# Attention: rows of maxima issued from ScalarE's queue, experts' chunks asked for in the last groups

## The chip, the cores and the metric

One Trainium2 chip, one core of it. The metric is the time on the device of one launch, in microseconds (us). TensorE does matmuls and transposes, VectorE and ScalarE elementwise work and reductions, GpSimd (POOL) some elementwise work and indirect transfers; SyncE (SP) issues nearly all DMAs. Each engine runs its own instructions in order and waits on semaphores for the others; all DMAs, whoever issues them, move through the same 16 DMA engines.

## The reference

Six layers in one launch on x of 4 images, 256 channels, 16 x 16: a deformable convolution block, a selective scan block, attention, a mixture of experts, causal attention, a second mixture of experts. What matters here is the attention, of which there are two, the second causal:

```
q, k, v = split(x @ w_qkv)              # 4 images x 16 heads, 256 tokens, head width 16
scores  = q @ k^T                       # causal in the second
attn    = softmax(scores / sqrt(16))
out     = (attn @ v) @ w_proj + b_proj
```

and that each attention is followed by 8 experts (hidden width 512 after the first attention, 1024 after the second), two of which are chosen for every token. The experts' weights are read from HBM in chunks of 1,536 KB: one per expert in the first mixture, two in the second. A ring in SBUF holds six chunks.

## The kernel before, in words

**Groups and units.** The 64 pairs of image and head are cut into 8 groups (`GROUPS`) of 8 pairs, a group into 4 units (`UNITS`) of 2 pairs. Unit i belongs to group i // 4. The softmax needs the maximum of each row of scores. A first pass computes scores (TensorE, line 1539, `scores_for_max`), whose maxima VectorE takes (line 1353; line 1348 in the causal attention). This pass runs ahead of the rest by up to two groups.

**Rows of maxima.** When the maxima of a group are complete, TensorE turns them (line 1549, `turn_maxima`) into a bank of PSUM; ScalarE writes their negative in bf16 (line 1439, `negate`), then VectorE writes the remainder (line 1359, `negate`). The result, two rows, is copied by two DMAs of 4 KB (8 pieces of 512 bytes each) into two extra rows of `stack_q` (line 1307, `load_max_rows`). There the second pass (line 1564, `scores_less_max`) subtracts them as part of the matmul. In the kernel before, GpSimd issues these two DMAs. Groups complete at units 2 (group 1), 4 (group 2), 8, 12, 16, 20 and 24 (group 7); group 0 before the first unit. Only the first unit of a group waits for the rows of that group, so those sent at unit 8 are needed at unit 12; those of group 1, sent at unit 2, are needed at unit 4.

**A unit.** For each unit TensorE computes the scores less the maxima, ScalarE exponentiates them (line 1463). In the causal attention GpSimd then zeroes the future (line 1313), in the same queue as the DMAs of line 1307. TensorE weighs the values for two units at a time (line 1584). In the first unit of a group ScalarE, after its exponential, takes the contexts of the group before out of PSUM (line 1444, `take_contexts`); TensorE turns them in the second unit (line 1595, `turn_contexts`), VectorE divides them (lines 1366 and 1368, `divide`), TensorE turns them back in the third (line 1602) and, for every second pair of groups, projects in the fourth (line 1612). The order of every engine's work is written out by hand in loops over `g` and `unit`.

**SyncE.** At the start of each group g, when its first unit's scores are done, SyncE issues one chunk of the experts' weights (line 1291, `prefetch`, line 1665), while there are chunks wanted: three in the first attention (groups 0 to 2), six in the second (groups 0 to 5). Then, in groups 1 to 4, it issues the 12 DMAs of 64 KB of the stacks of group g + 3 (line 1273, `load_stacks`). The first four groups' stacks are issued ahead of that loop (line 1283).

Of the kernel before, what the change touches and what calls it, by code (L numbers as in the profile page):

```python
# [1117 lines left out]
STACK = len(COMBOS) * HD  # L1118
MAXROWS = 2
GROUP = 8  # L1120
GROUPS = B * AH // GROUP
SLOTS_G = 4
# [25 lines left out]
def maxima_ahead(i):  # L1148


    catching_up = GROUP // 2
    first = FIRST_MAXIMA + 3 * min(i, catching_up) + 2 * max(i - catching_up, 0)
    return range(first, min(first + (3 if i < catching_up else 2), GROUP * GROUPS))


def maxima_complete(i):

    for g in range(1, GROUPS):
        if i > 0 and GROUP * g + GROUP - 1 in maxima_ahead(i - 1):
            return g  # L1160
    return 0


def attention(nc, sem, sbuf, psum, k, w, causal, tag, prefetch):
# [12 lines left out]
    with ExitStack() as ctx:  # L1177
# [16 lines left out]
        stack_q = sb("stack_q", [STACK + MAXROWS, SLOTS_G, GROUP, N], BF16)  # L1194
# [3 lines left out]
        negated = sb("negated", [GROUP, SLOTS_G, MAXROWS, N], BF16)  # L1198
# [26 lines left out]
        s_nh = sm("negated_high")  # L1225
        s_nl = sm("negated_low")
        s_mr = [sm("max_rows_even"), sm("max_rows_odd")]
# [31 lines left out]
        @block.sync  # L1259
        def _(sp):  # L1260
            for dst, src in ((wqkv, w["wqkv"]), (w_proj, w["w_proj"]), (b_proj, w["b_proj"])):
                sp.dma_start(dst[:], src).then_inc(s_w, 16)
            if causal:
                sp.dma_start(later[:], k.dram["later"]).then_inc(s_w, 16)

            sp.dma_start(stack_k[STACK:].rearrange("r s h n -> r (s h n)"), k.dram["ones16"]).then_inc(s_ones_rows, 16)

            def load_stacks(g):

                b, half = image_and_half(g)  # L1270
                for which, stack in enumerate((stack_q, stack_k)):
                    for c, combo in enumerate(COMBOS):
                        sp.dma_start(stack[c:STACK:len(COMBOS), g % SLOTS_G],
                                     parts[:, half, which, combo[which], N * b:N * b + N]).then_inc(s_st[g % SLOTS_G], 16)

            for g in range(SLOTS_G):
                b, t = image_and_half(g)
                for which in range(2):
                    for part, done in enumerate((s_hi, s_mid, s_lo)):
                        sp.wait_ge(done, 2 * t + which + 1)  # L1280
                        for c, combo in enumerate(COMBOS):
                            if combo[which] == part:
                                sp.dma_start((stack_q, stack_k)[which][c:STACK:len(COMBOS), g],
                                             parts[:, t, which, part, N * b:N * b + N]).then_inc(s_first[g], 16)
            sp.wait_ge(s_lo, SPLITS)

            for g in range(GROUPS - 1):

                sp.wait_ge(s_s2, UNITS * g + 1)
                prefetch(sp, g)  # L1290
                if g >= 1 and g + 3 < GROUPS:

                    load_stacks(g + 3)

        @block.gpsimd
        def _(pool):
            pool.memset(values[:, :, :, HD:], 1.0).then_inc(s_ones, 1)
            pool.wait_ge(s_ones, 1)
            pool.wait_ge(s_w, 16 * WEIGHTS)
            pool.wait_ge(ln.s_out, TT)  # L1300
            pool.tensor_tensor(k.t[:], k.t[:], b_proj[:].unsqueeze(1).broadcast_to([P, TT, C]), ALU.add).then_inc(s_bias, 1)

            def load_max_rows(g):
                pool.wait_ge(s_nl, g + 1)
                pool.wait_ge(s_nh, g + 1)
                for q in range(MAXROWS):
                    pool.dma_start(stack_q[STACK + q:STACK + q + 1, g % SLOTS_G], negated[:, g % SLOTS_G, q, :]  # L1307
                                   ).then_inc(s_mr[g % 2], 16)

            def zero_future(i):  # L1310
                pool.wait_ge(s_ex, i + 1)
                on_diagonal = exponentials(i).rearrange("p j (m n) -> p j m n", m=NT)[:, :, :, 0:P]
                pool.affine_select(on_diagonal, on_diagonal, [[0, 2], [0, NT], [1, P]], ALU.is_ge, 0.0, base=0,
                                   channel_multiplier=-1).then_inc(s_sel, 1)

            if causal:
                load_max_rows(0)
                for i in range(UNITS * GROUPS):
                    zero_future(i)
                    if maxima_complete(i + 1):  # L1320
                        load_max_rows(maxima_complete(i + 1))
            else:
                for g in range(GROUPS):
                    load_max_rows(g)

        @block.vector
        def _(dve):
# [75 lines left out]
        @block.scalar  # L1403
        def _(act):
            ln.deviation(act)

            def take_turned(i):
                act.wait_ge(s_ht, i + 1)
                act.activation(h_t[:, :, N * i:N * i + N], psum[:, 4 + i, :].rearrange("p (t n) -> p t n", t=CT),
                               ACT.Copy).then_inc(s_hto, 1)  # L1410

            def split(i):
                act.wait_ge(s_qk, i + 1)
                act.activation(part_of(i, 0), psum[:, split_bank(i), :], ACT.Copy).then_inc(s_hi, 1)
                act.wait_ge(s_r, i + 1)
                act.activation(part_of(i, 1), rest[:, i % 2, 0:BANK], ACT.Copy).then_inc(s_mid, 1)

            def take_values(i):

                act.wait_ge(s_v, i + 1)  # L1420
                act.activation(values[:, 2 * i:2 * i + 2, :, 0:HD],
                               psum[:, 4 + i, :].rearrange("p (a h d) -> p a h d", a=2, h=AH), ACT.Copy).then_inc(s_vo, 1)

            take_turned(0)
            take_turned(1)
            split(0)
            split(1)
            take_turned(2)
            take_turned(3)
            split(2)  # L1430
            split(3)
            take_values(0)
            take_values(1)
            for i in range(SPLITS // 2, SPLITS):
                split(i)

            def negate(g):
                act.wait_ge(s_mt, g + 1)
                act.activation(negated[:, g % SLOTS_G, 0, :], psum[0:GROUP, 0, 0:N], ACT.Copy, scale=-1.0).then_inc(s_nh, 1)

            def take_contexts(g):

                act.wait_ge(s_av, QUADS * (g + 1))
                act.activation(raw[:, g % 2, :], psum[:, 6 + g % 2, :], ACT.Copy).then_inc(s_raw, 1)

            def take_back(g):

                b, half = image_and_half(g)
                act.wait_ge(s_cb, g + 1)
                act.activation(ctxn[:, b % 2, half, :], psum[:, 6 + g % 2, 0:N], ACT.Copy).then_inc(s_cn, 1)  # L1450

            negate(0)
            for i in range(TT // 4, TT // 2):
                take_values(i)
            for g in range(GROUPS):
                for unit in range(UNITS):
                    i = UNITS * g + unit
                    if maxima_complete(i):
                        negate(maxima_complete(i))
                    act.wait_ge(s_s2, i + 1)  # L1460
                    if i >= 4:
                        act.wait_ge(s_av, i // 2 - 1)
                    act.activation(exponentials(i)[:, :, 0:WIDTH], psum[:, 2 + 2 * (i % 2):4 + 2 * (i % 2), 0:WIDTH],
                                   ACT.Exp, scale=HD ** -0.5).then_inc(s_ex, 1)
                    if unit == 0 and g >= 1:
                        take_contexts(g - 1)
                    if unit == 2 and g >= 1:
                        take_back(g - 1)
            take_contexts(GROUPS - 1)
            take_back(GROUPS - 1)  # L1470

# [189 lines left out]
def load_chunk(sp, k, weights, chunks, n, loaded):  # L1661

    place = CHUNK_COLS * (n % RING_CHUNKS)
    column = CHUNK_COLS * (n % chunks)
    sp.dma_start(k.ring[:, place:place + CHUNK_COLS], weights[n // chunks, :, column:column + CHUNK_COLS]).then_inc(loaded, 16)
# [612 lines left out]
def build(nc, k, out):  # L2278

    with ExitStack() as ctx:  # L2280
# [29 lines left out]

        def prefetcher(name, chunks, wanted, loaded):

            def prefetch(sp, i):
                if i < len(wanted):
                    load_chunk(sp, k, k.dram[name], chunks, wanted[i], loaded)
            return prefetch

        with nc.cleanup_on_exit():
# [39 lines left out]
```

## Time and profile before

| | |
|---|---|
| runs of the kernel, us | 1013.53, 1019.27, 1018.63 (median 1018.63) |
| the profiled execution, us | 1018.52 |
| its span, us | 1016.8 |
| mean granted clock of TensorE | 0.896 |
| busy share of the span | PE 82%, DVE 45%, ACT 30%, POOL 23% |
| DMA | 80.39 MB, mean 79 GB/s |

The span goes from the first to the last instruction of the profiled execution. Shares are averages over six layers with different limits; the two attentions lie between 257 and 388 us and between 577 and 694 us of the span. The granted clock is a fraction of TensorE's full speed; its two levels are 2.4 GHz (1.00) and 1.2 GHz (0.50).

### The profile page before, as it was taken

What the parts mean: (1) busy time and instruction counts of PE and PEld (TensorE: products, weight loads), DVE (VectorE), ACT (ScalarE), POOL (GpSimd) and SP (SyncE); (2) the same over time, 40 slices, a digit from 0 to 9 for tenths busy, and PEclk for the clock granted to TensorE, in tenths of its full rate; (3) what the DMA queues carried; (4) which work ended last, traced back from release to release, by engine and by line L of the source; (5) the groups of instructions that cost most, each with busy time, mean ns of one, the idle gap of its engine ahead of it and who ended that gap; (6) DMA issues with size and microseconds to landing.
All of it is one profiled execution on the core that took longest, in us unless ns stands there. A gap on an engine that the chain in (4) does not pass through costs nothing. (4 is left out here: it accounts for less than half of the span.)

```text
span 1016.8 us, 12888 instructions
## 1 busy us (share of the span) xinstructions
PE 837.7 (82%) x4088; PEld 538.6 (53%) x4089; DVE 452.6 (45%) x1165; ACT 301.3 (30%) x478; POOL 233.3 (23%) x314
## 2 busy tenths in 40 slices
PE   3769379899887986599999387876499999999993
PEld 2768237435743545366666344555356666666652
DVE  4974631698775645422222566645412121211213
ACT  3223235632244562012212144452021212222221
POOL 1150000573200100334433113340212211122110
PEclk8579677999898997699999597898699999999996
DMA  3000070000136503042111436832003007600003
GB/s 110 1 1 1 1 259 1 0 1 0 54 97 185 147 6 92 21 128 79 46 46 36 146 82 190 245 109 91 16 16 146 26 26 275 261 22 29 21 21 129
DMA packets 53621, 80.39 MB, mean 79 GB/s; under 512 B 10021, under 2 KB 45989, under 8 KB 50373
## 3 DMA queue, kind: packets, MB, share of 16 engines
q1 hardware_dynamic: 48040, 67.37, 20.5%
q0 software_dynamic: 5536, 12.46, 4.1%
q8 instruction: 24, 0.39, 0.2%
q14 instruction: 21, 0.16, 0.1%
HBM read 55.82 MB, written 11.27 MB: 66 GB/s over the span
## 5 line engine op out<-in xcount | busy, mean ns | idle before, releaser
L2096 PE MATMUL psum<-ring,f_x_t 128*128 x552 | 248.6, 593 | 1.3 <-DVE f_x_t L1961 1.3
L1954 DVE TENSOR_TENSOR f_gated<-f_silu,psum 128x512 f32<-128x512 f32 x69 | 47.5, 688 | 265.4 <-PE psum L2096 265.4
L2096 PEld LDWEIGHTS psum<-ring,f_x_t 128*128 128x128 f32 x552 | 99.5, 190 | 100.9 <-issue 100.8
L2110 PE MATMUL psum<-ring,f_gated_t 128*128 x552 | 130.7, 380 | 1.8 <-ACT f_gated_t L2020 1.8
L2110 PEld LDWEIGHTS psum<-ring,f_gated_t 128*128 128x128 f32 x552 | 101.2, 190 | 23.4 <-issue 12.7
L2020 ACT ACTIVATE f_gated_t<-psum 128x512 f32<-128x512 f32 x69 | 41.2, 597 | 235.0 <-PE psum L2103 231.5
L2016 ACT ACTIVATE f_silu<-psum 128x512 f32<-128x512 f32 x69 | 41.2, 597 | 116.5 <-PE psum L2096 109.8
L1114 PE MATMUL psum<-ident_sb 128*128 128x128 f32 x188 | 33.5, 347 | 30.8 <-PEq L2325 16.7
L1822 POOL COPY f_from_now<-f_from_row 128x1 uint32 (+1 forms) x48 | 9.0, 187 | 207.6 <-PE psum L2089 204.0
L1825 POOL DMA_INDIRECT f_xs<-rows_in,f_from_now x48 | 47.5, 989 | 36.5 <-POOL f_from_now L1822 36.5
L1834 POOL DMA_INDIRECT rows_out<-f_y,f_to_now x46 | 46.0, 1001 | 36.4 <-POOL f_to_now L1831 31.4
L1539 PE MATMUL psum<-a_stack_k,a_stack_q 96*128 96x256 bf16 (+1 forms) x256 | 43.3, 275 | 13.2 <-DVE a_maxima L1348 5.7
L1114 PEld LDWEIGHTS psum<-ident_sb 128*128 128x128 f32 x188 | 31.6, 260 | 32.7 <-issue 25.1
L1353 DVE TENSOR_REDUCE a_maxima<-psum 128x2 f32<-128x512 f32 x64 | 41.0, 686 | 11.9 <-PE psum L1539 11.9
L1564 PE MATMUL psum<-a_stack_q,a_stack_k 98*128 98x256 bf16 (+1 forms) x256 | 37.9, 275 | 8.8 <-DMA a_stack_q<-a_negated 7.3
L1307 POOL DMA_DIRECT2D a_stack_q<-a_negated x32 | 16.8, 530 | 120.5 <-DVE a_negated L1359 120.5
L1348 DVE CUSTOM_DVE_ANT_0 a_masked<-psum,a_later 128x128 bf16<-128x128 f32 (+1 forms) x128 | 38.1, 353 | 12.5 <-PE psum L1539 12.4
L719 POOL TENSOR_TENSOR u<-dtb,ring 128x512 f32<-128x512 f32 x32 | 40.4, 1268 | 13.2 <-ACT dtb L907 13.0
L2103 PE MATMUL psum<-ident_sb,f_gated 128*128 128x128 f32 x276 | 41.5, 273 | 1.3 <-DVE f_gated L1954 1.3
L1539 PEld LDWEIGHTS psum<-a_stack_k,a_stack_q 96*128 96x128 bf16 x256 | 20.9, 102 | 37.0 <-DVE a_maxima L1353 11.0
L802 DVE TENSOR_TENSOR_SCAN state<-psum,u 128x512 f32<-128x512 f32 x32 | 38.9, 1217 | 3.0 <-POOL u L719 3.0
L2103 PEld LDWEIGHTS psum<-ident_sb,f_gated 128*128 128x128 f32 x276 | 34.4, 141 | 9.1 <-DVE f_gated L1954 2.4
(295 smaller groups left out, 1259.1 us busy)
## 6 DMA issues: line engine op xcount, KB each, us to landing
ring<-in_f_experts SPq DMA_DIRECT2D x24, 1536.0 KB
a_stack_q<-a_parts SPq DMA_DIRECT2D x96, 64.0 KB, 2.0
a_stack_k<-a_parts SPq DMA_DIRECT2D x96, 64.0 KB, 2.0
rows_in<-h SPq DMA_DIRECT2D x4, 1024.0 KB, 5.8
ring<-rows_out SPq DMA_DIRECT2D x8, 512.0 KB, 5.8
a_wqkv<-in_a_wqkv SPq DMA_DIRECT2D x2, 768.0 KB, 4.4
x_in<-in_x SPq DMA_DIRECT2D x1, 1024.0 KB, 4.9
out<-x SPq DMA_DIRECT2D x4, 256.0 KB, 2.1
```

What stands on the lines that cost most here:

```text
L719: pool.tensor_tensor(u[:, i % DEEP, :], dtb[:, i % DEEP, :], x_perm[:, h, BANK * half:BANK * half + BANK], ALU.mult).then_inc(s_u, 1)
L1114: pe.matmul(bank[:, 0:P], k.ident_sb[:], k.ident_sb[:], start=True, stop=True)
L1353: dve.tensor_reduce(maxima[:, g, :, h], psum[:, i % 2, :].rearrange("p (t m) -> p t m", t=NT), AX_X, ALU.max).then_inc(s_mx, 1)
L1539: last = pe.matmul(out, stack_q[0:STACK, slot, h, P * t:P * t + P], stack_k[0:STACK, slot, h, 0:keys], start=True, stop=True)
L1825: pool.indirect_dma_start(out=xs[:, odd, :], out_offset=None, in_=k.rows_in, in_offset=bass.IndirectOffsetOnAxis(ap=from_now[:, odd:odd + ...
L1834: pool.indirect_dma_start(out=k.rows_out, out_offset=bass.IndirectOffsetOnAxis(ap=to_now[:, odd:odd + 1], axis=0), in_=y[:, odd, :], in_of ...
L1954: dve.tensor_tensor(gated[:, b, :], silu[:, b, :], psum[:, 2 * b + 1, :], ALU.mult).then_inc(s_g, 1)
L2016: act.activation(silu[:, b, :], psum[:, 2 * b, :], ACT.Silu).then_inc(s_si, 1)
L2020: act.activation(gated_t[:, b, :], psum[:, G_BANK + b, :], ACT.Copy).then_inc(s_gto, 1)
L2096: last = pe.matmul(psum[:, 2 * b + side, :], x_t[:, xb, t, :], k.ring[:, bass.ds(at + start, CHUNK)], start=(t == 0), stop=(t == CT - 1))
L2103: last = pe.transpose(psum[:, G_BANK + b, P * a:P * a + P], gated[:, b, P * a:P * a + P], k.ident_sb[:])
L2110: last = pe.matmul(psum[:, Y_BANK, 0:C], gated_t[:, b, P * a:P * a + P], k.ring[:, bass.ds(at + start, C)], start=(c == 0 and a == 0), sto ...
```

## The change

Two edits. First, the two DMAs of the rows of maxima are issued by ScalarE, directly after its `negate`, and no longer by GpSimd. For that ScalarE waits for VectorE's part (`s_nl`) before it issues them, and its exponential of that unit stands behind. This is so for group 0 ahead of the loop, and at units 2, 4, 8, 12, 16, 20 and 24, in both attentions. Second, SyncE asks for no chunk in groups 0 to 3; in groups 4, 5 and 6 it asks for a third of the wanted chunks each, one in the first attention and two in the second, and in group 4 behind the stacks of group 7.

```diff
@@ sync
                 sp.wait_ge(s_s2, UNITS * g + 1)
-                prefetch(sp, g)
                 if g >= 1 and g + 3 < GROUPS:
 
                     load_stacks(g + 3)
+                if g >= GROUPS - 4:
+                    prefetch(sp, g - (GROUPS - 4))
@@ gpsimd
-            def load_max_rows(g):
-                pool.wait_ge(s_nl, g + 1)
-                pool.wait_ge(s_nh, g + 1)
-                for q in range(MAXROWS):
-                    pool.dma_start(stack_q[STACK + q:STACK + q + 1, g % SLOTS_G], negated[:, g % SLOTS_G, q, :]
-                                   ).then_inc(s_mr[g % 2], 16)
...
             if causal:
-                load_max_rows(0)
                 for i in range(UNITS * GROUPS):
                     zero_future(i)
-                    if maxima_complete(i + 1):
-                        load_max_rows(maxima_complete(i + 1))
-            else:
-                for g in range(GROUPS):
-                    load_max_rows(g)
@@ scalar
+            def load_max_rows(g):
+                act.wait_ge(s_nh, g + 1)
+                act.wait_ge(s_nl, g + 1)
+                for q in range(MAXROWS):
+                    act.dma_start(stack_q[STACK + q:STACK + q + 1, g % SLOTS_G], negated[:, g % SLOTS_G, q, :]
+                                  ).then_inc(s_mr[g % 2], 16)
...
             negate(0)
+            load_max_rows(0)
             for i in range(TT // 4, TT // 2):
                 take_values(i)
...
                     if maxima_complete(i):
                         negate(maxima_complete(i))
+                        load_max_rows(maxima_complete(i))
                     act.wait_ge(s_s2, i + 1)
@@ build
         def prefetcher(name, chunks, wanted, loaded):
 
+            each = len(wanted) // 3
+
             def prefetch(sp, i):
-                if i < len(wanted):
-                    load_chunk(sp, k, k.dram[name], chunks, wanted[i], loaded)
+                for n in wanted[each * i:each * i + each]:
+                    load_chunk(sp, k, k.dram[name], chunks, n, loaded)
```

## Rows read from the trace of the kernel before

**Rows 1.** Busy time of each engine (x instructions), granted clock, DMA share, GB/s: two attentions.
```profile
288.00:388.00 100.00, 80.26 (x636) 46.59 (x635) 56.28 (x101) 49.34 (x68) 8.48 (x16) 0.95 0.36 102
577.00:694.00 117.00, 94.13 (x722) 60.64 (x722) 67.39 (x332) 51.76 (x86) 35.02 (x50) 0.88 0.51 148
```

**Rows 2.** Who waited for whom, TensorE, 304:366 us: total, times, longest.
```profile
PE psum L1564 <- DMA a_stack_q<-a_negated: 4.5, 2, 3.5
```

**Rows 3.** The same view, TensorE, 615:675 us.
```profile
PE psum L1564 <- DMA a_stack_q<-a_negated: 2.8, 2, 1.5
PE psum L1539 <- DMA a_stack_k<-a_parts: 1.2, 2, 0.7
```

**Rows 4.** Windows from one turning of maxima to the next, first attention, columns as rows 1.
```profile
309.44:318.49 9.05, 4.63 (x38) 2.29 (x39) 4.14 (x7) 2.30 (x3) 1.03 (x2) 0.95 0.55 190
318.49:328.77 10.28, 8.83 (x74) 4.71 (x73) 5.97 (x11) 5.33 (x7) 1.03 (x2) 0.83 0.75 225
328.77:337.98 9.21, 8.62 (x74) 4.47 (x73) 5.97 (x11) 5.33 (x7) 1.03 (x2) 0.87 0.90 256
...
357.22:365.37 8.15, 7.40 (x72) 4.28 (x73) 6.54 (x12) 5.20 (x7) 1.03 (x2) 1.00 0.01 1
```

**Rows 5.** The same windows in the second attention.
```profile
619.25:627.07 7.82, 5.68 (x39) 2.78 (x40) 4.10 (x25) 1.87 (x3) 2.33 (x4) 0.50 0.64 219
627.07:637.03 9.96, 7.98 (x75) 5.02 (x74) 5.71 (x35) 4.47 (x7) 3.59 (x6) 0.78 0.84 232
637.03:647.24 10.21, 8.88 (x74) 5.63 (x72) 5.71 (x35) 4.35 (x7) 3.59 (x6) 0.67 0.88 239
...
665.26:673.22 7.96, 6.18 (x72) 3.85 (x72) 6.21 (x36) 4.35 (x7) 3.59 (x6) 1.00 0.60 209
```

**Rows 6.** DMA issues, KB each, us to landing, window 309:320 us.
```profile
a_stack_q<-a_negated POOLq DMA_DIRECT2D x2, 4.0 KB, 5.6
```

**Rows 7.** DMA issues, the same columns, window 343:350 us.
```profile
a_stack_q<-a_negated POOLq DMA_DIRECT2D x2, 4.0 KB, 1.8
```

**Rows 8.** DMA queues, packets, MB, share of 16 engines, window 310.5:316.5 us.
```profile
q1 hardware_dynamic: 257, 1.62, 77.1%
```

**Rows 9.** SyncE's queue in order of time: start us, us, what.
```profile
309.84 9.22 SPq L1665 DMA_DIRECT2D ring<-in_f_experts  x2
...
350.77 5.00 SPq L1273 DMA_DIRECT2D a_stack_k<-a_parts  x6
...
388.21 0.43 SPq L1781 DMA_DIRECT2D f_iota_e<-in_iota_e  x1
388.69 0.42 SPq L1781 DMA_DIRECT2D f_iota_b<-in_iota_b  x1
```

**Rows 10.** SyncE's queue, second attention, the last stacks and the last chunk.
```profile
660.47 4.68 SPq L1273 DMA_DIRECT2D a_stack_k<-a_parts  x6
665.19 0.59 SPq L1665 DMA_DIRECT2D ring<-in_f_experts  x1
```

**Rows 11.** ScalarE in order of time at unit 16 of the first attention [idle <-releaser].
```profile
348.08 0.37 ACT L1439 ACTIVATE a_negated<-psum 8x256 bf16<-8x256 f32 x1 [2.69 <-PE psum L1549]
348.36 1.00 ACT L1463 ACTIVATE a_expo<-psum 128x1024 f32<-128x1024 f32 x1
349.26 0.57 ACT L1444 ACTIVATE a_rest<-psum 128x512 f32<-128x512 f32 x1
```

**Rows 12.** VectorE at the same unit.
```profile
348.49 0.41 DVE L1359 SCALAR_TENSOR_TENSOR a_negated<-psum,a_negated 8x256 bf16<-8x256 f32 x1 [0.88 <-ACT a_negated L1439]
```

**Rows 13.** TensorE: contexts turned; first scores of group 6.
```profile
349.92 0.62 PE L1595 MATMUL psum<-ident_sb,a_rest 128*128 128x128 f32 x4
...
364.41 0.60 PE L1564 MATMUL psum<-a_stack_q,a_stack_k 98*128 98x256 bf16 x4
```

**Rows 14.** TensorE in the second attention, values weighed at unit 18.
```profile
660.11 0.86 PE L1584 MATMUL psum<-a_expo,a_values 128*32 128x256 f32 x16 [0.18 <-POOL a_expo L1313]
```

**Rows 15.** A window of 3 us, first attention, columns as rows 1.
```profile
318.00:321.00 3.00, 3.00 (x23) 1.10 (x22) 0.41 (x1) 1.28 (x2) 0.73 (x2) 0.51 0.43 127
```

## The prediction

> **What bounds the kernel now.** The change touches the two attentions only, so I read the busy times by stage first: the two take about 100 and 117 us, TensorE is busy for 80.3 and 94.1 us of them, and the mean granted clock is 0.95 and 0.88 [rows 1]. Then the waits of TensorE inside the loops: it waited 4.5 us for the rows of maxima in the first attention (twice, the longest 3.5), 2.8 us in the second, and 1.2 us there for stacks [rows 2, 3]. Then the length of one group, from one turning of maxima to the next. A group without projection takes 8.15 us in the first attention when no transfer is in its way, at a full clock; those that begin at 318.49 and 328.77 take 10.28 and 9.21 at a mean clock of 0.83 and 0.87 [rows 4]. In the second the like are 7.96 against 9.96 and 10.21, at 0.78 and 0.67 [rows 5]. So the early groups lose time to DMA waits and to the lower of TensorE's two levels, which follows such waits: after the wait of 3.5 us the clock was 0.51 for 3 us [rows 2, 15].
>
> Why the rows of maxima come late is in the issues: beside a chunk the two DMAs of 4 KB landed 5.6 us after issue, beside stacks alone 1.8 us [rows 6, 7]. In 6 us SyncE's queue moved 1.62 MB, with all 16 engines busy 77.1% of it, so a chunk holds them for some 4.6 us [rows 8].
>
> **Step 1, chunks out of groups 0 to 3.** The first attention gets back the wait of 3.5 us before its second group, 10.28 - 8.15 = 2.1 and 9.21 - 8.15 = 1.1 [rows 2, 4]: 6.7 us. The second gets back 2.8 - 1.5 = 1.3 before its second group, 9.96 - 7.96 = 2.0 and 10.21 - 7.96 = 2.2 [rows 3, 5]: 5.5 us. Sum -12.2. The bounds: the waits alone, 4.5 + 2.8 + 1.2 = -8.5, if the lower clock stays; and -13.7, if the second attention's first window, all of it at 0.50, gives 1.5 us more [rows 5]. I take -12.2, since the undisturbed groups show the length that is left.
>
> The Trainium skill (DMA: Bandwidth & Descriptors, Queues, rings and completion order) says that each DMA engine goes round the queues it has work for, a packet at a time. By that the small rows should slip in between a chunk's packets; landings of 5.6 against 1.8 us don't look like it, unless a packet is a large part of a chunk. Its consequence is the third rival.
>
> **Step 2, two DMAs on ScalarE.** Unit 16 shows the chain. ScalarE's negation starts at 348.08, the exponential at 348.36, the contexts leave PSUM from 349.26 to 349.83 [rows 11]; TensorE turns them at 349.92 [rows 13]: slack 0.09. In the changed kernel ScalarE waits for VectorE's remainder, which ends at 348.49 + 0.41 = 348.90 [rows 12], 0.54 after the old start of the exponential, and then issues two DMAs. No row shows a DMA issued by ScalarE. Lower bound: the 0.05 us between two issues of SyncE (388.21 + 0.43 to 388.69); upper bound: a stack's issue with its gap, 0.64 (5.00 us for six is more still) [rows 9, 10]. The nearest is SyncE's small load, 0.43 + 0.05 = 0.48, but in four of six groups SyncE is issuing stacks at that moment; I take 0.55. The hold is 0.54 + 2 x 0.55 = 1.64, less the slack 1.55 us.
>
> I find no cover behind it. TensorE stands at the turning of contexts, and in its queue behind it the next scores for maxima; VectorE's division waits for that turning, with its next maxima queued behind; ScalarE's next exponential stands behind the taking of contexts. So TensorE, VectorE and ScalarE are all 1.55 us later at the next turning of maxima. It happens at units 4, 8, 12, 16, 20 and 24, six times in each attention: 12 x 1.55 = +18.6. Units 2 and the one ahead of the loop I cost at nothing: there the contexts aren't on the path, and the next copy or exponential on ScalarE waits for TensorE anyway; without that cover they cost 4 x 1.6 = 6.4. Bounds of the step: 12 x (0.54 + 0.1 - 0.09) = +6.6, and 12 x (0.54 + 1.28 - 0.09) = +20.8. Less than nothing is excluded: a wait and two issues can't make the exponential earlier.
>
> GpSimd loses 16 issues in each attention. In the second they stand ahead of the zeroing of the future, for which TensorE waited 0.18 us [rows 14]; but the exponential that feeds it is now 1.6 us later, so I count nothing.
>
> By the Trainium skill (Perfetto Trace Analysis, DMA Instruction — HWDGE) two sequencers share one descriptor generator under a lock, and the one that waits for it is held. No row here shows such a wait. By that rule each of ScalarE's DMAs could wait out one of SyncE's.
>
> **Step 3, chunks into groups 4 to 6.** In the second attention SyncE issues stacks until 665.15 and its next chunk follows at 665.19 [rows 10], when group 5 has begun. So the two chunks of group 4 and the two of group 5 are now asked for together, and two more a group later. Four chunks hold the DMA engines for 4 x 4.6 = 18 us [rows 8]; the rows of groups 6 and 7 are sent in that time and have some 6 to 7 us until they are needed (first attention: turned at 357.22, so sent about 358.9, and needed at 364.41 plus the hold [rows 4, 13]). Landing 5.6 us after issue costs nothing; if each of the two DMAs waits for a chunk of its own they land after about 10 us, 3 late. In the first attention two chunks stand where four do, about 1 late. Bounds 0 and +20 (all four chunks first). I take +4, near the landings seen. The blocks of experts begin only behind the attentions, at 388 and 694 [rows 1], and 18 us from 665 is 683, so the later chunks delay nobody.
>
> **Sum.** -12.2 + 18.6 + 4 = +10.4. The profiled execution took 1018.52, a tenth under the median of 1018.63; its span is 1016.8. Forecast 1018.5 + 10.4 = 1029 us.
>
> **Rivals.**
> 1. *The issue is cheap on ScalarE* (the other side). If a DMA costs it 0.05 and not 0.55 us, step 2 is +6.6; with step 1 at -13.7 and no collision late, the time is 1018.5 - 7.1 = 1011, and with -12.2 and +4 it is 1017. It decides below 0.12 us an issue: 12 x (0.45 + 2 x 0.12) = 8.2 is what steps 1 and 3 leave. For it: the chain has only 0.09 us of slack but all issues measured here are another engine's. Against: even SyncE's small loads take 0.42 us [rows 9]. Chance 0.22.
> 2. *Dearer still.* Each DMA of ScalarE waits 0.6 us for one of SyncE's in groups 1 to 4, 8 x 1.2 = +10; or the new gaps of 1.5 us put TensorE on its lower level, which doubles some 1 us of work in each of 12 groups. 1039 to 1045. The clock fell after a wait of 3.5 us [rows 15] but not in the undisturbed groups; a gap of 1.5 lies between. Chance 0.22.
> 3. *Queues take turns.* Then the slow landings come from GpSimd's own path; moving the rows to ScalarE cures them just as well, and step 3 is 0: 1025. Its contrary, strict order behind four chunks, gives +20: 1045. Chances 0.06 each; rows 6 and 7 speak against the first.
> 4. *The hold is absorbed somewhere I haven't seen* and only step 1 remains: 1006. Chance 0.06.
>
> **How the numbers follow.** The forecast, 1020 to 1038, has 0.38. A measurement of this kernel can tell about 1% from no change, that is 1008 to 1029. Faster by over 1%: rival 4 and the best third of rival 1, 0.13. Slower by over 1%: about 0.21 of the forecast, all of rival 2 and half of rival 3's cases, 0.49, cut to 0.47 for the unknown price of an issue. Within 1%: 0.40. The range leaves out rival 4 with the edge of rival 1, and the far end of rivals 2 and 3: 1009 to 1042.
>
> **What would show it.** In the changed trace: landings of the rows near 2 us in groups 1 to 5, no wait of the scores less maxima at groups 1 and 2, and a full clock there (step 1); two DMA rows on ScalarE between line 1439 and line 1463, their length, and a wait of line 1595 for line 1444 of about 1.5 us in twelve groups (step 2); groups of 9.7 us where 8.15 stood; a wait of groups 6 and 7 for the rows of maxima (step 3). The prediction is wrong if the exponential starts less than 0.8 us after its old place, or if undisturbed groups grow by less than 1 us.

## The result, and the profile after

The changed kernel takes 1035.3 us (median of four runs, 1034.3 to 1039.4) beside 1016.9 for the kernel before; the ratio is 1.019, with an interval of 1.015 to 1.024. The forecast was 1029: the sign and the hold on ScalarE came out, but of the 18.4 us only 10.4 were forecast, and the lower clock that follows the hold was not in the sum. The profiled executions, 1039.39 and 1018.52 us, lie 20.9 apart (the one of the changed kernel is the slowest of its four, with a mean granted clock of 0.890 where the others have 0.895 to 0.901), and the attentions hold it all: from the first turning of maxima (line 1549 before, 1546 after) to the experts' first load the first attention goes from 87.9 to 95.2 us and the second from 84.3 to 98.8, while the last mixture of experts takes 322.2 and 321.8.

ScalarE, then TensorE, at unit 16 of the first attention, in the changed kernel (start us, us, what, [idle before <-releaser]; compare [rows 11, 13]):

```profile
350.67 0.37 ACT L1427 ACTIVATE a_negated<-psum 8x256 bf16<-8x256 f32 x1 [2.69 <-PE psum L1546]
351.57 1.29 ACTq L1433 DMA_DIRECT2D a_stack_q<-a_negated  x2
352.96 1.02 ACT L1460 ACTIVATE a_expo<-psum 128x1024 f32<-128x1024 f32 x1 [1.92 <-PE psum L1561]
353.88 0.59 ACT L1439 ACTIVATE a_rest<-psum 128x512 f32<-128x512 f32 x1
```

```profile
352.07 0.60 PE L1561 MATMUL psum<-a_stack_q,a_stack_k 98*128 98x256 bf16 x4
354.53 0.66 PE L1592 MATMUL psum<-ident_sb,a_rest 128*128 128x128 f32 x4 [1.86 <-ACT a_rest L1439]
```

The exponential started 0.28 us after the negation and now starts 2.29 after it; between them are 0.53 of wait and 1.29 of issues. The idle time in the exponential's row is put down to TensorE's scores, but those of its unit were done by 349.5: a releaser that has long been done isn't the one; what ended last is the engine's own queue of DMAs. TensorE stands 1.86 us before it can turn the contexts. Over both loops this is the largest of its waits (total, times, longest); what else is listed are waits for VectorE's maxima and small ones of at most 1.0 us. No wait for the rows of maxima or for stacks is left, where there were 4.5, 2.8 and 1.2 us [rows 2, 3]. First attention 305:390, then second 615:702; of the eight waits in the first, six are at the turnings forecast and two behind them (0.17 and 0.72 us):

```profile
PE psum L1592 <- ACT a_rest L1439: 12.5, 8, 2.3
```

```profile
PE psum L1592 <- ACT a_rest L1439: 11.1, 6, 2.5
```

The groups, from one turning of maxima to the next (TensorE, its loads, VectorE, ScalarE, GpSimd busy, granted clock, DMA share, GB/s), answer to [rows 4, 5]. The second and third row are groups with and without projection at a full clock; the last two are groups with and without projection in the second attention, both below a full clock:

```profile
327.30:338.85 11.55, 9.00 (x72) 4.81 (x73) 6.07 (x11) 5.23 (x7) 0.00 (x0) 0.85 0.27 69
338.85:350.25 11.40, 8.81 (x80) 5.96 (x80) 6.16 (x11) 5.23 (x7) 0.00 (x0) 1.00 0.28 71
...
363.26:373.24 9.98, 7.42 (x72) 4.36 (x72) 6.63 (x12) 5.23 (x7) 0.00 (x0) 1.00 0.47 181
```

```profile
666.23:679.98 13.75, 10.53 (x81) 7.30 (x81) 6.30 (x36) 4.38 (x7) 2.55 (x4) 0.75 0.56 178
679.98:690.56 10.58, 7.60 (x73) 4.75 (x73) 6.22 (x36) 4.38 (x7) 2.55 (x4) 0.84 1.01 431
```

At a clock of 1.00 a group has grown from 8.15 to 9.98 us [rows 4], by 1.83: the hold and no more. Beside it stand groups of 11.55 and 13.75 us at 0.85 and 0.75, with TensorE busy for 9.00 us where the group of 9.98 has 7.42 for the same work. That is the second part of the loss, and the forecast had it only as a rival. SyncE's queue shows where the six chunks went: asked for from 673.46 on, behind the last stacks, four of them by 680.0 and the last two at 690.2.

```profile
669.41 4.00 SPq L1273 DMA_DIRECT2D a_stack_k<-a_parts  x6
673.46 17.50 SPq L1662 DMA_DIRECT2D ring<-in_f_experts  x6
```

### The profile page after: what moved, and what is told of

Same layout as the page of the kernel before. It is cut to its first block and busy times, and to the rows that moved or that the text cites. A ratio compares the mean times of both kernels' runs of the same rounds, so it can differ in the third digit from the quotient of the medians.

```text
span 1037.7 us, 12885 instructions
## 1 busy us (share of the span) xinstructions
PE 846.8 (82%) x4088; PEld 543.5 (52%) x4089; DVE 453.6 (44%) x1165; ACT 301.7 (29%) x478; POOL 216.4 (21%) x282
## 5 line engine op out<-in xcount | busy, mean ns | idle before, releaser
L1810 POOL TENSOR_TENSOR f_label_hot<-f_in_block,f_labels 128x192 bf16<-128x192 f32 x8 | 7.8, 1002 | 169.7 <-DVE f_in_block L1914 169.7
L1561 PE MATMUL psum<-a_stack_q,a_stack_k 98*128 98x256 bf16 (+1 forms) x256 | 40.5, 290 | 1.4 <-ACT a_values L1409 1.4
```

The lines of the kernel that those rows point to most:

```text
L1561: last = pe.matmul(psum[:, bank, col:col + N - first], stack_k[:, slot, h, P * m:P * m + P], stack_q[:, slot, h, first:N], start=True, sto ...
```

## The experiments

The theory was made from the traces of the two kernels, before the runs below. Theory *hold*: ScalarE's wait and two issues ahead of the exponential delay TensorE in twelve groups, and the gaps bring the lower clock with them. Rivals: the chunks in the last groups are the loss; the wait across engines and not the issue; the lower clock has another cause. Times are medians; the kernel before, on the same chip, was 1016.2, 1016.0 and 1015.6 us in the three sets (kernels 1 to 4, 5 to 8, 9 to 11).

**1. The queue alone.** The changed kernel, with the chunks as before the change. Here and below `...` marks lines left out within an edit, and the lines that only change how `prefetch` picks its chunks aren't shown.

```diff
+                prefetch(sp, g)
                 if g >= 1 and g + 3 < GROUPS:
                     load_stacks(g + 3)
-                if g >= GROUPS - 4:
-                    prefetch(sp, g - (GROUPS - 4))
```

> The rows of maxima are issued by ScalarE as in the changed kernel, but the chunks are asked for as before the change. Theory hold (the exponential stands behind ScalarE's wait and its two issues, 1.85 us in each of 12 groups, and the lower clock that follows takes the rest): the hold is all there, the chunks still delay the rows of the second group (up to 3.5 us), later waits are covered by the longer groups; 4 to 9 us slower than the changed kernel, 1039 to 1045. Rival late chunks (the six chunks in the last groups are what costs): this kernel loses that cost and lands at 1017 to 1027.

Measured 1045.8 us, ratio 1.026 (1.020 to 1.032), just above what was expected. The rival's 1017 to 1027 is far off, so the chunks aren't the loss. That the queue alone costs more than the whole change is likely and no more: three of its four runs took 1045 to 1047, one 1036.8, and the intervals of the two ratios overlap. Beside a chunk ScalarE's rows come late too: TensorE waits for them at group 1, 2.2 us in the first attention (305:390) and 1.2 in the second, where the changed kernel has no such wait.

```profile
PE psum L1560 <- DMA a_stack_q<-a_negated: 2.2, 1, 2.2
```

The rows of this wait were issued at 311.67. ScalarE's DMAs have a queue of their own in the trace, q10; all its 32 packets of these two rows start in 315.7:317.3, none in 311.67:315.7, while q1, SyncE's queue, moves the chunk (packets, MB, share of 16 engines):

```profile
q1 hardware_dynamic: 110, 1.35, 88.3%
```

```profile
q10 hardware_dynamic: 32, 0.01, 2.2%
```

**2. The chunks alone.** The other half of the change: GpSimd issues the rows, SyncE's lines are those of the changed kernel.

> GpSimd issues the rows of maxima as before the change; only the chunks are moved into groups 4 to 6. Theory hold: the waits of 4.5 and 4.0 us and the lower clock behind them go, 1003 to 1008, with groups of 8.1 us in the first attention. Rival late chunks: slower than before, 1020 or more, with waits for the rows in groups 6 and 7. Rival (the slow landings are GpSimd's own path): landings stay at 5 us and the time at 1015 to 1019.

Measured 1013.0 us, ratio 0.996 (0.994 to 0.998): a gain, but 5 us less than expected. The early groups of the first attention came out as forecast (8.14 and 8.55 us at a clock of 1.00). In the second the first two windows keep the lower clock, 0.51 and 0.78, though no wait for rows or stacks stands there. The last groups now wait for the rows of maxima. TensorE's waits, second attention, 669:696:

```profile
PE psum L1565 <- DMA a_stack_q<-a_negated: 4.4, 2, 3.5
```

and one group, in which TensorE waited 1.8 us for stacks, stands at a clock of 0.75:

```profile
638.48:651.94 13.46, 10.64 (x80) 7.19 (x81) 5.71 (x35) 4.36 (x7) 3.60 (x6) 0.75 0.28 71
```

**3. ScalarE's issues moved behind the contexts.** The changed kernel with

```diff
                         negate(maxima_complete(i))
-                        load_max_rows(maxima_complete(i))
+                        if i == 2:
+                            load_max_rows(1)
...
                     if unit == 2 and g >= 1:
                         take_back(g - 1)
+                        if g + 1 < GROUPS:
+                            load_max_rows(g + 1)
```

> The changed kernel, but from group 2 on ScalarE issues the two rows in the third unit of the group, after it has taken the contexts back, and not ahead of the exponential of the first unit; the rows are sent some 4 us later. Theory hold: TensorE's wait of 1.85 us at the turning of contexts goes in all twelve groups, 1004 to 1012, with perhaps a short wait for the rows at each group's start. Rival (any DMA issue on ScalarE costs its 1.3 us wherever it stands, since ScalarE is full): 1025 or more.

Measured 1027.5 us, ratio 1.011 (1.008 to 1.014): a miss by 15 us, in the range that was given to the rival. The trace speaks against the rival all the same. The wait for the contexts is gone, as the theory has it; but rows sent 4 us later land late, above all beside the chunks, which I hadn't priced: TensorE waits 6.2 us for them in the first attention and 13.0 in the second. TensorE's waits in the second attention, 615:702:

```profile
PE psum L1564 <- DMA a_stack_q<-a_negated: 13.0, 5, 6.2
...
PE psum L1595 <- ACT a_rest L1439: 0.7, 1, 0.7
```

**4. The wait without the issues.** Kernel 2, with ScalarE waiting for VectorE's remainder.

```diff
                         negate(maxima_complete(i))
+                        act.wait_ge(s_nl, maxima_complete(i) + 1)
```

> GpSimd issues the rows and the chunks are late (as in the kernel with only the chunks moved), but ScalarE waits for VectorE's remainder before its exponential and issues nothing. It parts the hold into wait and issue. Theory hold, by its parts (0.54 of wait, 2 x 0.64 of issue, 0.09 of slack): 12 x 0.5 = 6 us over the kernel with only the chunks moved, 1009 to 1014, TensorE's wait at the turning of contexts about 0.6 us. Rival (it is the wait across engines, not the issue, that costs): as slow as the changed kernel, 1030 or more.

Measured 1016.4 us, ratio 1.000 (0.998 to 1.001), 3.4 over kernel 2, where 6 was expected, and above the interval expected. TensorE's wait for the contexts (305:390) is 0.42 us at each plain turning, where about 0.6 was expected; a part of it comes back, as the longer groups leave the rows more time (3.1 us of waiting where kernel 2 had 4.1 there).

```profile
PE psum L1597 <- ACT a_rest L1445: 3.3, 6, 0.9
PE psum L1566 <- DMA a_stack_q<-a_negated: 3.1, 2, 2.9
```

**5. TensorE kept busy in the gap.** The changed kernel, with 12 transposes of the identity, into a bank that is overwritten later, ahead of the wait for the contexts in groups 1 to 6.

```diff
+            def keep_busy(g):
+                if g >= 2:
+                    pe.wait_ge(s_cn, g - 1)
...
+                square_identity(pe, k, psum[:, 6 + g % 2, :], 12)
...
                     if unit == 1 and g >= 1:
+                        if g < GROUPS - 1:
+                            keep_busy(g)
                         turn_contexts(g - 1)
```

> The changed kernel, in which TensorE runs 12 transposes of the identity (about 1.5 us at the higher clock, into a bank that is overwritten later) in the second unit of groups 1 to 6, where it would stand and wait for the contexts. They fill the gap of 1.85 us and change nothing of the order. Theory clock (the gaps bring TensorE to its lower level in the groups that follow, which the trace of the changed kernel shows as 0.75 to 0.87): the clock returns to 1.00, groups 4 and 5 of the second attention shrink from 13.5 to about 11, and the kernel gains 8 to 15 us on the changed kernel, 1020 to 1028. Rival (the lower clock has another cause, and the groups are long by the hold alone): the fillers cost or give nothing, 1033 to 1040.

Measured 1030.9 us, ratio 1.014 (1.010 to 1.018): outside the interval expected, 4.4 us less than the changed kernel. The clock is 1.00 in the whole first attention, and in the second but for its first three windows (0.83, 0.51 and 0.83), but twelve transposes took some 2.6 us and overran the gap: a group with projection took 11.99 where the changed kernel has 11.40.

**6. One row each.** The changed kernel, with the second row issued by GpSimd, with a semaphore of its own.

```diff
@@ scalar
-                for q in range(MAXROWS):
+                for q in range(1):
@@ gpsimd
+            def load_second_row(g):
+                pool.wait_ge(s_nl, g + 1)
+                pool.wait_ge(s_nh, g + 1)
+                pool.dma_start(stack_q[STACK + 1:STACK + 2, g % SLOTS_G], negated[:, g % SLOTS_G, 1, :]
+                               ).then_inc(s_mr2[g % 2], 16)
...
```

> The changed kernel, but ScalarE issues one of the two rows and GpSimd the other. Theory hold, by its parts: ScalarE's hold is shorter by one issue of 0.64 us, TensorE's wait at the turning of contexts 1.2 instead of 1.85 us, 12 x 0.64 = 7.7 us less, and more if the clock is lost only behind the longer gap: 1020 to 1028. Rival (the first DMA of ScalarE carries the cost, the second is cheap): 1032 or more.

Measured 1024.1 us, ratio 1.008 (1.005 to 1.010), as expected: 11.2 us less than the changed kernel, 12 x 0.64 = 7.7 for the issues, the rest by the clock, if theory and kernel 9 hold. Its gaps are 1.20 us and not 1.86, and the clock of all full groups of the first attention is 1.00 (9.32 us without projection, 10.73 with it); in the second three of five are at 1.00. ScalarE at unit 16 (344.51 its negation): the hold is shorter by one issue.

```profile
344.51 0.37 ACT L1440 ACTIVATE a_negated<-psum 8x256 bf16<-8x256 f32 x1 [2.69 <-PE psum L1559]
345.41 0.63 ACTq L1446 DMA_DIRECT2D a_stack_q<-a_negated  x1
346.14 1.02 ACT L1473 ACTIVATE a_expo<-psum 128x1024 f32<-128x1024 f32 x1 [1.26 <-PE psum L1595]
```

**7. Rows by SyncE**, but for group 0's; chunks when the last rows have landed.

```diff
                 sp.wait_ge(s_s2, UNITS * g + 1)
+                sp.wait_ge(s_nh, g + 2)
+                sp.wait_ge(s_nl, g + 2)
+                for q in range(MAXROWS):
+                    sp.dma_start(stack_q[STACK + q:STACK + q + 1, (g + 1) % SLOTS_G], negated[:, (g + 1) % SLOTS_G, q, :]
+                                 ).then_inc(s_mr[(g + 1) % 2], 16)
...
```

> SyncE issues the rows of groups 1 to 7, ahead of each group's stacks, GpSimd those of group 0; all chunks are asked for when the rows of the last group have landed. SyncE's 12 stacks take 7.6 us or more of a group of 8; with the wait for the remainder (1.5 us) and 1.3 us for the rows its queue needs 10.5 us a group in groups 1 to 4. Theory (SyncE's queue becomes the bound): waits for stacks in groups 2 to 5 of both attentions, 5 to 12 us more than with GpSimd's issues, 1008 to 1018. Rival (its queue has room): as fast as the kernel with the chunks last, 1000 to 1006.

Measured 1018.9 us, ratio 1.003 (1.001 to 1.005), one above the interval expected and 9.5 us slower than kernel 8, which differs from it only in who issues the rows. SyncE becomes the bound; TensorE in the second attention (615:702):

```profile
PE psum L1545 <- DMA a_stack_k<-a_parts: 6.6, 3, 2.8
```

It also prices the disputed DMA on another engine. All 28 on SyncE, then all 32 on ScalarE in the changed kernel (ns, min/median/max):

```profile
L1294 SPq DMA_DIRECT2D a_stack_q<-a_negated x28: 623/686/732, 310.2 to 674.4; - x28
```

```profile
L1433 ACTq DMA_DIRECT2D a_stack_q<-a_negated x32: 627/627/1234, 302.3 to 692.5; - x32
```

**8. Rows by GpSimd, all chunks when the last rows have landed.** Kernel 2 with

```diff
-                if g >= GROUPS - 4:
-                    prefetch(sp, g - (GROUPS - 4))
+            sp.wait_ge(s_mr[(GROUPS - 1) % 2], 16 * MAXROWS * (GROUPS // 2))
+            for i in range(3):
+                prefetch(sp, i)
```

> GpSimd issues the rows as before the change; all chunks are asked for only when the rows of the last group have landed, so that no row is sent beside a chunk. Theory collision (rows sent beside a chunk land some 4 us later, whoever asks for them): the waits of 3.5 us before the last group of both attentions and of 0.9 us before the one before it, which the kernel with only the chunks moved shows, are gone, and their lower clock: 5 to 10 us faster than that, 1002 to 1008. Rival (they are late for another reason, or the chunks now delay the experts' block): 1011 or more.

Measured 1009.4 us, ratio 0.994 (0.992 to 0.995), 3.6 less than kernel 2, where 5 to 10 were expected, and above the 1008 of the theory's range: the waits for rows are gone. The second attention still has its wait of 1.8 us for stacks and a group of 13.39, and the router waits 1.6 us for a small load behind six chunks.

**9. Eight transposes.** Kernel 5 with

```diff
-                square_identity(pe, k, psum[:, 6 + g % 2, :], 12)
+                square_identity(pe, k, psum[:, 6 + g % 2, :], 8)
```

> As the kernel with fillers, but 8 transposes instead of 12: one took 0.22 us, so that twelve took 2.7 us and ran 0.6 us past the gap in each of 12 groups; eight take 1.8 and fit it. Theory clock: a clock of 1.00 in the loops as with twelve, and 12 x 0.6 = 7 us less than with twelve, 1022 to 1026; groups 3 and 4 of the first attention at 11.4 us. The difference to the changed kernel, 10 to 13 us, is then the price of the lower level alone. Rival (the clock costs little): 1029 or more.

Measured 1026.0 us, ratio 1.009 (1.006 to 1.013), at the upper end of what was expected. But for the first windows of either attention (down to 0.50) the loops have the changed kernel's hold at the higher clock: 11.40 as in its undisturbed group, and 10.98 in the second attention where it had 13.75.

```profile
349.63:361.03 11.40, 10.60 (x96) 7.83 (x97) 6.73 (x12) 5.23 (x7) 0.00 (x0) 1.00 0.47 128
...
660.73:671.71 10.98, 9.50 (x96) 7.34 (x97) 6.31 (x36) 4.38 (x7) 2.55 (x4) 1.00 0.51 141
```

So the lower level costs the changed kernel 1035.3 - 1026.0 = 9.3 us by the medians (12.0 by the profiled executions). The two medians are of different sets, in which the kernel before took 1016.9 and 1015.6; by the ratios it is 10.

**10. Stacks one unit earlier.** Kernel 8 with

```diff
-                sp.wait_ge(s_s2, UNITS * g + 1)
+                sp.wait_ge(s_s2, UNITS * g)
```

> The kernel with the chunks last, but SyncE begins a group's stacks when the last unit before it has its scores, not the first unit of the group (the slot it fills is free by then). In the kernel with the chunks last one group of the second attention waits 1.8 us for stacks and takes 13.4 us at a clock that falls behind it. Theory (once the groups take 7.7 to 8.8 us, SyncE's 12 issues, 7.6 us and 2 to land, are the next bound): the wait goes, the group takes 9 to 10 us, 3 to 5 us less than the kernel with the chunks last, 1003 to 1007. Rival (the long group has another cause): 1008 or more.

Measured 1006.4 us, ratio 0.991 (0.988 to 0.994). It is as expected, 3.0 us less than kernel 8. No wait for rows or stacks is left in either loop, and the group of 13.39 is one of 9.02. The lower clock of the second attention's first two windows is still there, 0.52 and 0.77, so the waits for rows and stacks aren't its cause; what is wasn't tried.

```profile
316.77:324.92 8.15, 7.41 (x73) 4.29 (x74) 5.97 (x11) 5.21 (x7) 1.03 (x2) 1.00 0.38 95
...
627.83:635.49 7.66, 6.19 (x72) 3.87 (x72) 5.62 (x35) 4.36 (x7) 3.56 (x6) 1.00 0.42 105
635.49:644.51 9.02, 7.65 (x80) 5.44 (x81) 5.71 (x35) 4.36 (x7) 3.56 (x6) 1.00 0.37 92
```

**11. The first chunk a group earlier.** Kernel 10, with `prefetch` taking the first and last chunk wanted.

```diff
+            sp.wait_ge(s_mr[(GROUPS - 2) % 2], 16 * MAXROWS * ((GROUPS - 2) // 2 + 1))
+            prefetch(sp, 0, 1)
             sp.wait_ge(s_mr[(GROUPS - 1) % 2], 16 * MAXROWS * (GROUPS // 2))
-            for i in range(3):
-                prefetch(sp, i)
+            prefetch(sp, 1, None)
```

> The same, and the first of the chunks is asked for as soon as the rows of the group before the last have landed, the others when those of the last group have. It ends the six chunks of the second attention 4.6 us earlier; the router of the experts waited 1.6 us for a small load behind them. Theory: 0 to 3 us less than the kernel with early stacks, 1001 to 1006. Rival (the chunk meets the rows of the last group again): 1008 or more, with a wait for the rows of the last group.

Measured 1006.0 us, ratio 0.990 (0.987 to 0.992), not to be told from kernel 10. The router's wait is gone, but TensorE waited 1.1 and 0.7 us for the rows of maxima again: both the gain and the rival's collision are in the trace, and by the medians they cancel. Both beat the kernel before by 1%, and by the medians the changed one by 2.8%.

## Why the prediction was right or wrong

**Step 1, chunks out of the early groups: right, with luck in the second attention.** It said -12.2, of which 6.7 and 5.5. In kernel 8 the first attention, from its second turning of maxima on, takes 71.7 us against 78.4 before: -6.7. In the second the gain shows only when the stacks come in time: kernel 10 has 70.0 us there (612.57 to 682.56), against 75.3 before (619.25 to 694.58): -5.3. Its terms came out otherwise than forecast: 1.4, 1.1 and 2.55 us in the first three windows and 0.3 in the rest, where 1.3, 2.0 and 2.2 stood, for the group of 9.96 shrank only to 8.83 and kept its lower clock (0.77). That the chunks delayed the rows is shown by kernels 1, 2 and 8. These figures are of single traces; by the medians kernel 10 gains 9.1 us in all, and in the kernel with rows by ScalarE the move of the chunks gave 1045.8 - 1035.3 = 10.5 us.

**Step 2, the hold: right in kind and place, short in size.** TensorE waits 1.86 us in the plain groups where 1.55 was forecast, 12 x 1.86 = 22.3 against 18.6 us, and above the step's upper bound of 20.8. The exponential starts 2.01 us later than it did, 0.54 + 1.28 + 0.19, and the last term, the time between VectorE's end, the issues and the exponential, wasn't priced. The term that was mis-sized most is the issue: 0.64 us each with its gap, my upper bound, and not 0.55, which is 0.18 of the 0.31 us. I had taken the nearest row by size, SyncE's small load of 0.43; SyncE takes 0.62 to 0.73 for this same DMA (kernel 7), as for its stacks. The sharing of SyncE's time wasn't it. That nothing covers the hold is shown by the groups at a full clock, +1.83 each, and that wait and issue both count by kernels 4 and 6. The issues at unit 2 cost nothing, as forecast: the window behind them, 5.58 us, is as long as in kernel 2.

The Trainium skill (Perfetto Trace Analysis, DMA Instruction — HWDGE) would have let each of ScalarE's DMAs wait for one of SyncE's. The trace doesn't bear that out as a rule: the median of the 32 is their minimum, 627 ns, though SyncE was issuing beside 20 of them; only one, the first, took 1234.

**Step 3, chunks beside the last rows: right as a mechanism, covered in the changed kernel.** It said +4; there is no wait for rows at all. Kernel 2 shows the collision (waits of 0.5 and 3.6 us in the first attention and 0.9 and 3.5 in the second), and kernel 8 its price, 3.6 us. In the changed kernel the rows are as late, but they are needed later: those sent at 681.30 have their packets in 685.2:687.3, up to 5.9 us after issue, and are needed after 8.3; those sent at 691.88 have them in 695.9:698.4, up to 6.5 us after issue, and are needed after 7.0. Kernel 2 needs the same rows after 5.4 and 3.9 us. So the longer groups, by the hold and by the lower clock, cover the delay, in the last group just so. I had counted the slack of the hold but not the whole of it. The windows 681.3:685.2 and 685.2:687.3 (beside stacks, at 351.57, the last packet starts within 2.3 us):

```profile
q1 hardware_dynamic: 150, 1.65, 99.0%
```

```profile
q1 hardware_dynamic: 79, 0.91, 102.1%
q10 hardware_dynamic: 32, 0.01, 1.7%
```

**The clock: the step that was missing.** I gave the lower level as a part of rival 2 and let the forecast keep the higher one. At eight of the twelve gaps the granted clock falls to 0.50, in the gap or up to 1.7 us behind it, and stays there for 3.4 us or more. Kernels 5 and 9 show that filling the gap brings it back: 9.3 us. Kernel 6, with gaps of 1.20 us, has it at 1.00 in eight of ten full groups.

The corrected sum: -12.0 + 22.3 + 9.3 + 0 = +19.6, against 1035.3 - 1016.9 = +18.4 by the medians and +20.9 by the profiled executions. Rival 1 fell with the 0.64 us; rival 4 with the groups of 9.98. Both halves of rival 3 fell by the packets of q10. GpSimd's own path isn't the cause, for ScalarE's rows are as late beside a chunk (kernel 1). Nor do they stand behind all chunks asked for: four were at 681.30, from 673.46 on, some 18 us of transfer by the prediction's 4.6 each, and the rows went through 3.9 us after issue, in which q1 moved 1.65 MB, about one chunk. That is no turn after every packet either.

## What to carry to other kernels

A DMA issue isn't free on an engine that computes: price it by the same transfer's shape on any queue, with the wait for its producer, and look at what stands behind it in that engine's order. Move it to an engine whose queue is empty at that moment, or change what it collides with; here the second alone gave the gain. And price a new gap on TensorE twice, once for its length and once for the lower clock behind it; here gaps of 1.86 us had that second price and gaps of 1.20 us hardly.

## What the runs showed of the hardware

The DMA of 4 KB in 8 pieces holds ScalarE for 0.63 us, SyncE for 0.69 and GpSimd for 0.52. Issued by GpSimd, it lands 1.8 us after issue beside stacks but 5.6 beside a chunk [rows 6, 7]; issued by ScalarE beside chunks, its first packet starts 3.1 to 4.5 us after issue, beside stacks 1.3 to 1.4. At the gap of 1.86 us TensorE fell to 1.2 GHz for 3.4 us or more in eight of twelve groups, not in all: the group from 338.85 to 350.25 has the same gap and a clock of 1.00. What tells the two apart wasn't tried. Work without use in the gap (8 transposes) made the whole kernel 9 us faster.
